# A graph layer on one core: V projected one batch ahead of the aggregation, with double-buffered V and a reordered start

## The reference

```
h      = relu(layernorm(x))                 # over the 1024 nodes of a channel
q, k   = wq . h, wk . h                     # one number per node each
scores[m, n] = leaky_relu(q[n] + k[m], 0.01)
att    = softmax(scores, over n)
agg    = h @ att^T                          # 512 channels by 1024 nodes
out    = x + relu(adj @ agg + bm)           # adj is 512 by 512
```

## Time and profile before

| | |
|---|---|
| runs | 2120.24, 2122.78, 2122.8 us |
| profiled execution | 2123.36 us, its span 2121.6 us |
| TensorE | 2055.9 us busy, 97%, 11312 matmuls |
| VectorE | 1640.8 us busy, 77% |
| ScalarE | 1219.2 us busy, 57% |
| POOL | 390.6 us busy, 18% |
| DMA | 271.51 MB, mean 128 GB/s |
| mean granted clock of TensorE | 0.993 |

### The profile page before, as it was taken

How to read it: one execution, slowest core, us unless ns; L and a number is a source line. 1 busy time by engine, 2 the same in 40 slices (tenths; PEclk the granted TensorE clock), 3 DMA queues, 4 the chain that set the end, 5 groups by cost and what they waited for, 6 DMA issues and landing times.

```text
span 2121.6 us, 35163 instructions
## 1 busy us (share of the span) xinstructions
PE 2055.9 (97%) x11312; PEld 960.5 (45%) x11312; DVE 1640.8 (77%) x3661; ACT 1219.2 (57%) x1873; POOL 390.6 (18%) x266
## 2 busy tenths in 40 slices
PE   4599999999999999999999999999999999999999
PEld 2244444444444444444444444444444444444444
DVE  6777788778888778787777887787887777877753
ACT  3565555655646665556655556555566655566543
POOL 0012211112212112111122211122111122111221
PEclk9799999999999999999999999999999999999999
DMA  5265544555544565444565445555445654445541
GB/s 169 91 149 140 125 106 144 134 149 139 117 102 152 128 156 135 100 123 140 139 148 120 118 129 136 144 139 118 105 149 129 154 134 104 120 143 139 114 100 40
DMA packets 178624, 271.51 MB, mean 128 GB/s; under 512 B 87648, under 2 KB 87648, under 8 KB 170336
## 3 DMA queue, kind: packets, MB, share of 16 engines
q1 hardware_dynamic: 178528, 270.59, 50.1%
HBM read 202.91 MB, written 67.63 MB: 128 GB/s over the span
## 4 chain that ended last, share of the span: by engine, by line
PE 80%; DVE 10%; issue 7%; DMA 1%; ACT 1%; SPq 0%; DVEq 0%; POOLq 0%
PE mix L338 15%; PE mix L339 15%; PE mix L340 15%; PE mix L319 10%; PE mix L321 10%; PE mix L320 10%; DVE den_out L612 4%; DVE p_ring L632 4%; PE small L302 2%; DVE p_lo L639 2%; DMA ab_rows<-ab_col 1%; DMA wm_nat<-in_adj_dram 0%; ACT v_hi L426 0%; DVE v_lo L644 0%; DMA ab_row<-ab_rows 0%
## 5 line engine op out<-in xcount | busy, mean ns | idle before, releaser
L338 PE MATMUL mix<-p_hi,v_hi 128*128 128x512 f16 x2048 | 777.2, 379 | 10.1 <-DVE p_lo L639 10.1
L339 PE MATMUL mix<-p_lo,v_hi 128*128 128x512 f16 x2048 | 776.9, 379 | 0.0
L340 PE MATMUL mix<-p_hi,v_lo 128*128 128x512 f16 x2048 | 776.8, 379 | 0.0
L736 POOL TENSOR_TENSOR res<-res,y 128x512 f32<-128x512 f32 x256 | 386.1, 1508 | 1710.2 <-ACT y L433 1710.2
L414 ACT ACTIVATE p_ring<-ab_row,cols 128x512 f32<-128x512 f32 x512 | 349.4, 692 | 181.4 <-DVE p_lo L639 155.4
L632 DVE SCALAR_TENSOR_TENSOR p_ring<-ab_row,cols,p_ring 128x512 f32<-128x512 f32 x512 | 376.7, 747 | 77.1 <-ACT p_ring L414 46.5
L319 PE MATMUL mix<-wmT_hi,h_hi 128*128 128x512 f16 x1024 | 389.2, 380 | 0.0
L321 PE MATMUL mix<-wmT_hi,h_lo 128*128 128x512 f16 x1024 | 389.1, 380 | 0.0
L320 PE MATMUL mix<-wmT_lo,h_hi 128*128 128x512 f16 x1024 | 389.1, 380 | 0.0
L612 DVE SCALAR_TENSOR_TENSOR den_out<-den_row,cols 128x512 f32<-128x512 f32 x512 | 371.6, 762 | 0.0
L422 ACT ACTIVATE p_hi<-p_ring 128x512 f16<-128x512 f32 x512 | 303.2, 592 | 87.3 <-DVE p_ring L632 69.9
(11 more groups left out here) (56 smaller groups left out, 782.2 us busy)
## 6 DMA issues: line engine op xcount, KB each, us to landing
xs<-in_x_dram SPq DMA_DIRECT2D x128, 512.0 KB, 6.1
res<-in_x_dram SPq DMA_DIRECT2D x256, 256.0 KB, 3.5
out_dram<-res SPq DMA_DIRECT2D x256, 256.0 KB, 2.5
den_row<-den_rows SPq DMA_DIRECT2D x32, 1024.0 KB, 4.6
ab_row<-ab_rows SPq DMA_DIRECT2D x32, 1024.0 KB, 6.8
wm_nat<-in_adj_dram SPq DMA_DIRECT2D x1, 1024.0 KB, 9.7
den_rows<-cols SPq DMA_DIRECT2D x32, 8.0 KB, 1.6
ab_rows<-ab_col SPq DMA_DIRECT2D x32, 8.0 KB
```

Of the source, the lines that this page charges most:

```text
L338: pe.matmul(ps[:, :], v_hi[:, nt, chans], p_hi[:, hf, nt, :], start=(nt == 0), stop=False)
L339: pe.matmul(ps[:, :], v_hi[:, nt, chans], p_lo[:, hf, nt, :], start=False, stop=False)
L340: mm = pe.matmul(ps[:, :], v_lo[:, nt, chans], p_hi[:, hf, nt, :], start=False, stop=(nt == NT - 1))
L736: pool.tensor_tensor(res[:, k, :], res[:, k, :], y[:, k % 2, :], ALU.add).then_inc(s_add, 1)
```

## The change

- `v_hi` and `v_lo` get two buffers, picked by the parity of the batch.
- TensorE's `period(b)` runs the units of b and then `v_phase(b + 2)`: tile 0 of V, the q/k product of the same batch, tiles 1 to 3, the spread of the q max, tiles 4 to 7. The first tile waits for all four h_lo of its own batch. The units' waits on v_lower change with it. In the next to last period no V phase stands between the units of batch 30 and those of batch 31.
- `v_slots` becomes `half_0(b, v, stats_of)`: half 0 of p for b + 1, beside the v_lower of b + 2, and after slots 4 to 7 the statistics of batch b + 3, one channel tile each. q_head and q_tail stand one slot earlier.
- VectorE's half 1 keeps six denominators between the weights; the last two come after them. Its loop makes 13 passes. In the next to last period all denominators and row_scales come ahead of half 1.
- ScalarE: normalise 0 and 1 ahead of relu 5, 2 and 3 ahead of relu 6. In the next to last period half 0 comes ahead of relu 7.
- The start: ScalarE issues the loads of the weights, SP those of x. x of batch 1 goes into `x_second`, which lies in `res`, and does not wait for batch 0. Batch 0's h32 is made by VectorE (`h_full_first`). V of batches 0 and 1 are both made ahead of the first unit. a and b of batch 0 are not sent through DRAM but spread by 16 transposes on TensorE and copied from PSUM by ScalarE and VectorE. The scaling of the weights on POOL and their transposes go tile by tile.

The core of the diff:

```diff
@@ buffers
-        v_hi = sb("v_hi", [P, NT, O], F16)
-        v_lo = sb("v_lo", [P, NT, O], F16)
+        v_hi = sb("v_hi", [P, 2, NT, O], F16)
+        v_lo = sb("v_lo", [P, 2, NT, O], F16)
+        x_second = res[:, :, :].rearrange("p (c h) n -> p c (h n)", h=2)
@@ SP
             for c in range(CT):
-                load_x(first, c)
...
+                sp.dma_start(xs[:, c, :], channels(first, c)).then_inc(s_x[c], 16)
+            sp.wait_ge(s_w, 16)
             for c in range(CT):
-                load_x(second, c)
+                sp.dma_start(x_second[:, c, :], channels(second, c)).then_inc(s_x1[c], 16)
             write_den_rows(first)
             load_den_rows(first)
+            for c in range(CT):
+                sp.dma_start(xs[:, c, :], channels((1, 0), c)).then_inc(s_x[c], 16)
             for k in range(U):
+                sp.wait_ge(s_h32, CT + k // 2 + 1)
                 load_residual(first, k)
-            write_ab_rows(first)
-            load_ab_rows(first)
-            for c in range(CT):
-                load_x((1, 0), c)
@@ TensorE
             def v_tile(b, nt):
+                if nt == 0:
+                    pe.wait_ge(s_hlo, cnt(b, CT, CT))
...
-            def unit(b, k):
+            def unit(b, k, one):
-                if k < MIX:
-                    pe.wait_ge(s_vlo[k % 2], cnt(b, NT // 2, (k + MIX) // 2 + 1))
+                if k >= MIX:
+                    pe.wait_ge(s_y[k % 2], cnt(b, U // 2, (k - MIX) // 2 + 1))
+                elif one:
+                    pe.wait_ge(s_vlo[k % 2], cnt(nxt(b), NT // 2, (k + MIX) // 2 + 1))
...
+            def spread_first_ab():
+                pe.wait_ge(s_dn, D_OPS)
+                for r in range(2):
+                    for t in range(NT):
+                        mm = pe.transpose(first_rows[2 * r + t // 4][:, (t % 4) * P:(t % 4 + 1) * P],
+                                          ab_col[:, r, t:t + 1].to_broadcast([P, P]), ident[:, :])
+                mm.then_inc(s_a1, 1)
+            def v_phase(b):
+                for nt in range(NT):
+                    if nt == 1:
+                        project_qk(b)
+                    if nt == 4:
+                        spread_qmax(b)
+                    v_tile(b, nt)
             def period(b, one, two):
                 for k in range(U):
-                    unit(b, k)
-                if one:
-                    for nt in range(NT):
-                        if two and nt == 2:
-                            project_qk(nxt(b, 2))
-                        if two and nt == 5:
-                            spread_qmax(nxt(b, 2))
-                        v_tile(nxt(b), nt)
+                    unit(b, k, one)
+                if two:
+                    v_phase(nxt(b, 2))
...
             project_qk(second)
-            spread_qmax(second)
+            for nt in range(NT):
+                if nt == 1:
+                    spread_qmax(second)
+                if nt == 5:
+                    spread_first_ab()
+                v_tile(second, nt)
@@ ScalarE
                 if two:
                     normalise(nxt(b, 2), 0)
+                    normalise(nxt(b, 2), 1)
                 relu(b, 5)
                 if two:
-                    normalise(nxt(b, 2), 1)
                     normalise(nxt(b, 2), 2)
+                    normalise(nxt(b, 2), 3)
                 relu(b, 6)
+                if one and not two:
+                    half_0(nxt(b), None)
+                relu(b, 7)
                 if two:
-                    normalise(nxt(b, 2), 3)
-                relu(b, 7)
-                if one:
-                    v_slots(nxt(b), two)
+                    half_0(nxt(b), nxt(b, 2))
@@ VectorE
+            def h_full_first(ct):
+                dve.wait_ge(s_ln, LN_OPS)
+                wait(dve, s_hlo, ct - 1)
+                dve.tensor_scalar(h32[:, ct % 2, :], xs[:, ct, :], ln_scale[:, 0, ct:ct + 1],
+                                  ln_shift[:, 0, ct:ct + 1], ALU.mult, ALU.add).then_inc(s_h32, 1)
...
-            def v_slots(b, two):
+            def half_0(b, v, stats_of, first_tile=0):
                 weight(b, 0)
                 for nt in range(NT):
                     if nt < NT - 1:
                         weight(b, nt + 1)
-                    v_lower(b, nt)
+                    if v and nt + first_tile < NT:
+                        v_lower(v, nt + first_tile)
                     p_lower(b, nt)
-                    if two and nt == 2:
-                        q_head(nxt(b))
-                    if two and nt == 4:
-                        q_tail(nxt(b))
+                    if v and not first_tile and nt == 1:
+                        q_head(v)
+                    if v and not first_tile and nt == 3:
+                        q_tail(v)
+                    if stats_of and nt >= NT - CT:
+                        statistics(stats_of, nt - NT + CT)
-            def period(b, one, two):
+            def period(b, one, two, three):
+                if one and not two:
+                    for nt in range(NT):
+                        denominator(nxt(b), nt)
+                    row_scales(nxt(b))
                 weight(b, NT)
                 for nt in range(NT):
                     if nt < NT - 1:
                         weight(b, NT + nt + 1)
-                    if one:
+                    if two and nt < NT - 2:
                         denominator(nxt(b), nt)
                     p_lower(b, NT + nt)
-                if one:
+                if two:
+                    denominator(nxt(b), NT - 2)
+                    denominator(nxt(b), NT - 1)
                     row_scales(nxt(b))
-                if two:
-                    for ct in range(CT):
-                        statistics(nxt(b, 2), ct)
+                    if at(b, first):
+                        for ct in range(CT):
+                            statistics(nxt(b, 2), ct)
                     normaliser(nxt(b, 2))
                     for ct in range(CT):
                         h_lower(nxt(b, 2), ct)
                 if one:
-                    v_slots(nxt(b), two)
+                    half_0(nxt(b), nxt(b, 2) if two else None, nxt(b, 3) if three else None)
```

More of the change, by code:

```diff
@@ L123, in gnn_layer @@
         wmT_ps = mix
-        assert CT == 4
+        first_rows = ring + [small]
+        assert CT == 4 and NT == 8
         qk_ps = small[:, 0:4 * NT].rearrange("p (t j) -> p t j", j=4)
         qmax_ps = small[:, 128:256]
-        s_wv = sem("wq_wk_bm_loaded")
+        s_wr = sem("wq_wk_rows_loaded")
+        s_wv = sem("wq_wk_bm_columns_loaded")
         s_w = sem("wm_loaded")
         s_x = [sem(f"x_loaded_{c}") for c in range(CT)]
+        s_x1 = [sem(f"x1_loaded_{c}") for c in range(CT)]
         s_xr = [sem(f"x_residual_loaded_{k}") for k in range(U)]
@@ L153, in gnn_layer @@
         s_ar = sem("ab_rows_loaded")
+        s_a1 = sem("first_ab_rows_spread")
         s_lk = sem("leak_ready")
@@ L169, in nxt, with at @@
             return (b[0] + j // 2, j % 2)
+        def at(b, batch):
+            return isinstance(b[0], int) and b == batch
         def cnt(b, per, n):
@@ L310, in v_tile @@
             def v_tile(b, nt):
-                if nt < MIX:
-                    wait(pe, s_y[nt % 2], cnt(b, U // 2, (nt + MIX) // 2 + 1 - U // 2))
+                if nt == 0:
+                    pe.wait_ge(s_hlo, cnt(b, CT, CT))
+                if nt < MIX and at(b, second):
+                    pe.wait_ge(s_vlo[nt % 2], (nt + MIX) // 2 + 1)
+                elif nt < MIX:
+                    wait(pe, s_y[nt % 2], cnt(b, U // 2, (nt + MIX) // 2 + 1 - U))
                 else:
@@ L444, in v_slots @@
                         leak(b, nt + 2)
-                    if two and nt == 5:
-                        exponentials(nxt(b))
+                    if v and not first_tile and nt == 5:
+                        exponentials(v)
             def period(b, one, two):
@@ L484, in _ @@
                 normalise(second, ct)
-            leak(first, 0)
-            leak(first, 1)
-            for nt in range(NT):
-                p_upper(first, nt)
-                if nt < NT - 2:
-                    leak(first, nt + 2)
-                if nt == 3:
-                    exponentials(second)
+                v_upper(first, CT + ct)
+            exponentials(second)
+            for nt in range(5):
+                v_upper(second, nt)
+            copy_first_a(0)
+            copy_first_a(1)
+            half_0(first, second, 5)
             period((0, 0), True, True)
@@ L682, in _ @@
             normaliser(first)
+            h_full_first(0)
+            h_full_first(1)
             scaled_weights()
-            for ct in range(CT):
-                h_lower(first, ct)
+            h_lower_first(0)
+            h_lower_first(1)
+            h_full_first(2)
+            h_full_first(3)
+            h_lower_first(2)
+            h_lower_first(3)
             weights_lower()
@@ L688, in _ @@
             q_tail(first)
```

(27 more changed lines are left out.)

126 lines of the change are left out of this document (64 added, 62 removed).

## The result

The changed kernel took 2130.5 us, the median of five runs (2128.78 to 2136.63), beside 2120.4 (2119.74 to 2122.8) for the kernel before in the same five rounds. The ratio is 1.0048 [1.0037, 1.006]: slower, by half of a per cent. The forecast was 2135 in a range of 2109 to 2159. The profiled execution is the median one, 2130.5 us with a span of 2128.7, so 7.1 us above the span before (2121.6). The profiled execution before, 2123.36 us, lay 3 us above the median of these rounds, so 3 of the 10 us between the medians are not in the two profiles.

What follows compares the result with a forecast made beforehand. TensorE was taken to bound the steady part, busy throughout but for 10.9 us of stalls, with idle time in the head. 2123.4 - 16.5 (head) + 18 (steady) + 11 (tail) = 2135.9, so 2135 as median; range 2109 to 2159.

Steps and rivals of the forecast that it cites:

- Head: Start up to V of batch 2: V2 at 131.8 instead of 148.3, a gain of 16.5 us, bounds 13 and 20.
- a drop of its clock: In the head, after about 3.2 us of TensorE idle behind V0's tiles, its clock falls to the lower level, 1.1 us.
- Steady part: Periods between head and tail: 30 us of stalls less 1 of slack, against 10.9 now, so 18 us lost.
- Half 0 cannot start before this: VectorE's half 0 must wait for the ab rows read back from DRAM; ring of 63.3 us, 65.7 with the loop head.
- rival (a): Steady part: DMAs are short and only the h chain binds, 65.2 us against 63.87; total 2122, no change; chance 0.16.
- The DMA terms: Ab rows' trip through DRAM in the steady part: 12.4 us taken for the write, 7.2 for the read.
- the ring through DRAM: Steady part: half 0, half 1, ab write, read and first weight in turn, 63.9 us or 66.3, 130.2 per pair.
- None before L338 in unit 4: Sign of being right: TensorE's waits list none before L338 in unit 4, as the stalls there go.
- VectorE idles 5 to 6 us before L632 at each half 0: Sign of being right, steady part: VectorE idles 5 to 6 us at each half 0, released by ab_row.
- The waits for h_lo: Sign of being right: TensorE waits for h_lo before L319 once per pair of batches, over 1 us each.
- The loop head: VectorE's return to its loop head, every second batch: the stall of 2.43 us stays, over 12 returns.
- Tail: Before batch 31's units: ab write stands behind store 3, first weight at 46.0, loss 11 us, bounds 8 and 13.

Runs made afterwards that it cites:

- experiment 2: Changed kernel with V tile 0 waiting for h_lo one channel tile at a time, not all four: 2114.32 us, ratio 0.9974 to the kernel before.
- experiment 4: Changed kernel with batch 2's statistics moved from behind row_scales of batch 1 to between v_lower of batch 1's first V tiles: 2125.14 us, ratio 1.002.
- experiment 1: Changed kernel writing the ab rows to DRAM for batch 1 alone, later batches rereading them (wrong scales): 2121.26 us, ratio 1.0002.
- experiment 5: Kernel before with only VectorE's order changed: statistics in the V phase, last two denominators of half 1 behind its weights: 2119.16 us, ratio 0.999.
- experiment 6: Changed kernel with VectorE's loop of 13 passes written out, same instructions in the same order: 2128.62 us, ratio 1.0034.
- experiment 3: Changed kernel with batch 31's ab rows written before store 0 instead of after store 3: 2124.44 us, ratio 1.0013.
- experiment 7: Changed kernel with h_lo wait per channel tile, batch 31's ab write ahead of store 0, and batch 2's statistics under V1: 2103.0 us, ratio 0.9918.

## Why the prediction came out right, step by step

**Head: right in its time, with two errors that meet.** V2 was put at 131.8 and began at 132.12. Within it V0 began at 31.12 and not at 29.7. The statistics waited for the x loads four times, and ln_shift ended at 16.77 instead of 14.5:
```profile
5.71 1.29 DVE L592 BATCH_NORM_STATS2 stats<-xs 128x6 f32<-128x512 f32 x2 [5.71 <-DMA xs<-in_x_dram]
...
16.80 1.53 DVE L628 TENSOR_SCALAR h<-xs,ln_scale,ln_shift 128x1024 f32<-128x1024 f32 x2
```
Before, the same loads had landed for the first statistics at 4.10. The weight's 1 MB took 12.2 us to land where it took 9.7, so both moved beside each other and each was slower. That fits the Trainium skill, "DMA: Bandwidth & Descriptors", section "Issuing engines are not separate DMA queues": an engine of its own saves the issue, not the transfer. The last row shows h_full at 0.73 us from start to start, 0.81 each (two in 1.53), not at the 0.9 of the sum; the second pair took 1.81, so this gave only 0.3 us back. The Trainium skill, "VectorE: DVE Perf Modes", section "Mode 2×_2P — use both read ports for one tensor", has such an operation at twice the rate of a tensor_tensor. The trace agrees that it is the faster one, but 0.81 is two thirds of h_lower's 1.22, not half. From V0 on, the chain took 101.0 us where 102.1 were reckoned.

What failed in size is the gain, 13.9 and not 16.5. The step "a drop of its clock" was counted for the first hole only. The wait of 4.5 us ahead of V2 was predicted, and the clock falls there too: V2's first tile and the q/k product took 6.47 us (132.12 to 138.59) where they take 4.19. That is 2.3 us, and experiments 2 and 4 gave it back by shortening the wait.

**Steady part: right in sign, wrong in cause.** The step that failed is "Half 0 cannot start before this, and once it starts late its tiles are all there, so it has no slack of its own: the ring is ... 63.3". Half 0 does start with the ab rows, but its slots 4 to 7 carry the statistics and its v_lower wait for V tiles, so its end is set by the V tiles: 26.36 us after V's start whether the first weight comes at 3.8 us or, in experiment 1, at 1.0. The length of half 0 was right, 21.4 us in experiment 5; what failed is that it starts late enough to matter. It would have to start more than 26.4 - 21.4 = 5.0 us after V. In the changed kernel V itself waits for h_lower, and the first weight was later than that in two of the 28 periods, by 0.5 us at most. What binds is the loop that the prediction worked out as rival (a), 65.2 us with the loop head in it and so 62.8 in every other period. It measured 64.38 in the period above and about that in all of them, because the 2.4 us of the loop head, once per pair, gave way to two times 1.0 in each period. The stalls are 17.9 us and the loss 7.05, not 18 (rival (a) put them at 16 and 5).
The DMA terms were too long as well: the write landed after 11.5 us and the read after 5.9, where 12.4 and 7.2 were taken.
```profile
DMA to landing us min/median/max: 10.9/11.5/12.2
DMA to landing us min/median/max: 5.2/5.9/8.7
```
So even by the prediction's own terms the ring through DRAM comes to 21.5 + 22.1 + 11.5 + 5.9 + 0.7 = 61.7, inside the period. "None before L338 in unit 4" held. "VectorE idles 5 to 6 us before L632 at each half 0" did not: 3.9 us at 913.48, 2.2 at 976.13, and 5 or more in three of the 28. The waits for h_lo came in every period, most of them 0.3 to 0.4 us, not once per pair with over 1 us.

**The loop head: wrong.** The prediction had the 2.43 us stay in 12 passes. They are gone; instead, single instructions are longer, by 49 us in all over the 28 periods. Such instructions were there before too, one per period and 0.5 to 0.7 us each, 15.5 us in all. Experiment 5 has two per period of 1.0 us and no wait at the loop head either, so the edits on VectorE alone bring the exchange. The Trainium skill, "Runtime: NRT & Kernel Launch", section "Instruction fetch mechanics", ties such a stall to a taken branch. Before, the trace agreed. After, the branch is still taken and the wait is gone, and the long instructions, in experiment 6 too, stand in straight code, so the rule does not reach them.

**Tail: right in mechanism, 13.6 and not 11.** The write stood behind store 3, as the step said; experiments 1 and 3 show it by taking the hole away. The hole was 9.3 us with 2.6 of small gaps, near the 11 of the sum. On top comes the clock again: nine matmuls at the lower level after the hole, 1.8 us more.

So 2135.9 was reckoned for the profiled execution and 2130.5 came: gain in the head 2.6 too large, tail 2.6 too small, first period 0.3, and the steady part 11 too large. That the total came so near is in part luck: about half of the 11 us too many in the steady part was made up by what the head and the tail had too few, most of that (4.1 us) two clock terms left out. With 7 in place of 18 and the rest as reckoned the sum would have been 2123.4 - 16.5 + 7 + 11 = 2125, no clear change.

## What to carry to other kernels

When a ring of waits is added up, ask of each station whether it is paced by its own inputs: a stage that starts late but ends with its last input has taken up the lateness, and the ring through it does not bind. Put a wait on the piece that is needed next, not on the whole set: waiting for one h_lower at a time, instead of all four, was worth 16 us here (2130.5 to 2114.32). Look then for the ring next in length: in experiment 7 the one through DRAM took 3.5 us back. Every predicted idle time of TensorE of several us needs its clock term beside it.

## What the runs showed of the hardware that was not expected

- An idle time of 4.5 us of TensorE was followed by eleven matmuls at the lower clock level and one of 9.1 us by nine, 2.3 and 1.8 us lost; after idle times of 0.96 and 1.44 us (experiment 2) and of 1.78 (experiment 7) there was none.
- With the first V tile at 31.1 us in both, one execution had 16 matmuls of the first V tiles at the lower level and another 23, and its first unit began 1.8 us later.
- VectorE instructions of 0.74 and 0.2 us took 1.0 us more at the same two places of nearly every period, with the loop and without it.
- An fp32 tensor_scalar of 128 by 1024 took 0.8 us in three of four cases (1.10 in the fourth), where h_lower, with two tensors of the same columns, takes 1.22.
